# Attention's second product: weighed exponentials stationary, 17 columns of values and ones moving

## The reference, cut to what matters

```python
q, k, v = split_heads(h @ Wq.T), split_heads(h @ Wk.T), split_heads(h @ Wv.T)   # 8 heads of 16
scores = jnp.einsum('bhqd,bhkd->bhqk', q, k) / math.sqrt(HEAD_DIM)
scores = scores + jnp.log(adjacency + 1e-06)[:, None, :, :]
attn = jax.nn.softmax(scores, axis=-1)
out = jnp.einsum('bhqk,bhkd->bhqd', attn, v).transpose(0, 2, 1, 3).reshape(b, n, HIDDEN)
x = x + out @ Wo.T + bo            # h is the layer norm of x
```

## Time and profile before

| | |
|---|---|
| median of three runs | 2202.75 us (2199.62 to 2203.97) |
| the profiled execution | 2199.14 us, its span 2197.4 us |
| PE, DVE, ACT, POOL busy over the span | 77%, 56%, 38%, 35% |
| attention, steady part | 910 to 1270 us of the span, granted clock 1.00 |
| in 910 to 1270: PE, DVE, ACT busy | 273.12, 302.84, 163.89 us of 360 |

### The profile page before, as it was taken

The page is one execution under the profiler, slowest core; times in us unless marked ns, Lnnn a source line. Parts: engine busy times, 40 slices in busy tenths (PEclk is TensorE's granted clock), DMA queues, the critical chain, the costliest instruction groups (busy, mean ns, idle before and its releaser), DMA issues. The chain is left out here.

```text
span 2197.4 us, 44487 instructions
## 1 busy us (share of the span) xinstructions
PE 1691.7 (77%) x13042; PEld 1410.7 (64%) x13042; DVE 1234.2 (56%) x4542; ACT 824.8 (38%) x2531; POOL 764.8 (35%) x1118
## 2 busy tenths in 40 slices
PE   5567999987649966777777779935999957872996
PEld 4555777765639964566666657725999945661663
DVE  5673333349856756688888855512222248862543
ACT  2333444433336642344444434302655523330000
POOL 3430000013326745200000027773554424543565
PEclk8888999998879985799999989967999967665887
DMA  2100000001014420000000021114777752203331
GB/s 70 57 29 8 1 1 1 1 13 34 28 33 130 124 57 0 1 0 0 0 0 0 0 71 48 48 52 129 207 208 206 206 141 81 64 23 66 98 79 46
DMA packets 156776, 129.84 MB, mean 59 GB/s; under 512 B 27852, under 2 KB 131055, under 8 KB 156610
## 3 DMA queue, kind: packets, MB, share of 16 engines
q1 hardware_dynamic: 136130, 99.30, 16.6%
q0 software_dynamic: 13568, 25.90, 3.5%
q10 hardware_dynamic: 6912, 2.65, 0.6%
HBM read 96.51 MB, written 33.35 MB: 59 GB/s over the span
## 5 line engine op out<-in xcount | busy, mean ns | idle before, releaser
L1429 ACT ACTIVATE FEAT<-BANKS,EXP 128x128 f32<-128x128 f32 x544 | 155.0, 368 | 181.4 <-PE BANKS L1406 181.4
L1047 ACT ACTIVATE EXP<-BANKS,NEGMAX 128x128 f32<-128x128 f32 x512 | 139.0, 383 | 191.5 <-DVE NEGMAX L1059 191.5
L195 PE MATMUL BANKS<-ident,WA 128*128 128x128 f32 x256 | 62.8, 392 | 163.2 <-DVE WA L189 163.1
L1360 POOL DMA_INDIRECT scratch_made<-FEAT x136 | 130.2, 958 | 147.8 <-DVE FEAT L1489 144.8
L195 PEld LDWEIGHTS BANKS<-ident,WA 128*128 128x128 f32 x256 | 42.9, 199 | 174.2 <-DVE WA L189 136.8
L412 PE MATMUL BANKS<-FEAT,ident 128*128 128x256 f32 x588 | 150.0, 383 | 0.0
L1489 DVE TENSOR_TENSOR FEAT<-BANKS,B2BC 128x128 f32<-128x128 f32 x136 | 39.7, 292 | 194.5 <-PE BANKS L1415 194.5
L1406 PE MATMUL BANKS<-FEAT 128*128 128x128 f32 x1088 | 146.3, 278 | 2.4 <-DMA FEAT<-in_L_ffn_W1p 1.2
L1415 PE MATMUL BANKS<-AUX,FEAT 128*128 x1088 | 143.9, 275 | 0.4 <-ACT FEAT L1429 0.4
L1074 DVE RECIPROCAL WD<-BANKS 128x256 f32<-128x256 f32 x64 | 112.5, 1758 | 55.4 <-PE BANKS L1018 55.4
L1162 POOL DMA_INDIRECT scratch_sent<-FEAT,POS x128 | 123.7, 966 | 40.6 <-issue 37.8
(11 more groups left out here) (361 smaller groups left out, 4556.4 us busy)
## 6 DMA issues: line engine op xcount, KB each, us to landing
FEAT<-in_L_ffn_W1p SPq DMA_DIRECT2D x136, 256.0 KB
EXP<-in_L_ffn_W SPq DMA_DIRECT2D x128, 128.0 KB, 2.1
FEAT<-scratch_sent SPq DMA_DIRECT2D x136, 64.5 KB
STAGE<-in_adj SPq DMA_DIRECT2D x32, 256.0 KB, 3.0
EXP<-scratch_made SPq DMA_DIRECT2D x32, 256.0 KB
FEAT<-scratch_sent SPq DMA_DIRECT2D x96, 65.5 KB, 1.9
X<-in_x SPq DMA_DIRECT2D x16, 256.0 KB, 3.3
scratch_sent<-NONE SPq DMA_DIRECT2D x48, 65.5 KB, 3.9
```

What stands on the lines that cost most here:

```text
L195: last = pe.transpose(tile(ps, k), tile(src, k), ident[:])
L1047: last = act.activation(tile(EXS[:, par], 4 * k + n), tile(PS[j], c), ACT.Exp, bias=NEGMAX[:, par, 4 * k + n:4 * k + n + 1])
L1360: pool.indirect_dma_start(out=made2, out_offset=bass.IndirectOffsetOnAxis(ap=XI_I[:, t % R_IN, H:ROW2], axis=0), in_=YO[:, t % R_OUT, :], ...
L1429: last = act.activation(tile(HR[:, t % R_H], c), tile(PS[2 + t % 2], c), ACT.Gelu, bias=BT[:, c, t:t + 1])
```

## The change

`product` now holds a head's PTA tile (128x128) stationary and streams 17 columns past it: 16 of the values and one of ones, which VP now holds. The result is token-major, [128 tokens, 8 heads x 17] in ACC (136 columns of PS[7]). `divide` takes the reciprocal of 8 columns and multiplies with a broadcast. Since `output` needs features on the partitions, `flip` (PE) transposes the divided result into PS[6], `turned` (ACT) copies it to OTT, and `output` is one matmul with the plain Wo, into another part of PS[7]. Wo is loaded in one DMA and no longer in eight, and its zeroed buffer goes. The pipeline has a depth of five in place of three, and all steps are written out. The transposes no longer wait for `add`; `product` does. The rest of the diff adapts counts of waits.

```diff
-                for chunk in range(NC):
-                    for tile_at in range(HC):
-                        h = HC * (tile_at % 2) + 2 * chunk + tile_at // 2
-                        sp.dma_start(WoP[HP * tile_at:HP * tile_at + HD, chunk, :],
-                                     a["L2_gnn_Wo_T"][h * HD:(h + 1) * HD, :]).then_inc(s.w, 16)
+                sp.dma_start(WoT[:], a["L2_gnn_Wo_T"]).then_inc(s.w, 16)
...
+        HD1 = HD + 1
+        VP = EXP[:, 4 * SW:4 * SW + 2 * HEADS * HD1].rearrange("p (a h d) -> p a h d", a=2, h=HEADS)
+        OT = WC[:, :, 0:H]
+        OTT = WC[:, :, H:2 * H]
+        INV = WD[:, :, 0:HEADS]
+        ACC = PS[7][:, 0:HEADS * HD1].rearrange("p (h d) -> p h d", h=HEADS)
+        FLIP = PS[6][:, 0:T]
+        OUT = PS[7][:, 256:256 + H]
+        head_of = lambda slot: HC * (slot % 2) + slot // 2
...
                 def qk(i, par, half):
                     reused(pe, s.qk, i, 1)
+                    if i >= 4:
+                        pe.wait_ge(s.oc, i - 3)
...
                 def scores(i, par, half):
                     pe.wait_ge(s.qk, i + 1)
-                    reused(pe, s.ex, i, 1, 2)
                     for j in range(HC):
                         rows = slice(HP * j, HP * (j + 1))
+                        if i >= 1 and j % 2 == 0:
+                            pe.wait_ge(s.ex, 2 * (i - 1) + j // 2 + 1)
...
                 def transpose(i, par, half):
                     for k in range(2):
-                        if not isinstance(i, int) or i >= 1:
-                            pe.wait_ge(s.pTa, 2 * i)
-                            if not isinstance(i, int) or i >= 2:
-                                pe.wait_ge(s.x1, i - 1)
+                        if i >= 1:
+                            pe.wait_ge(s.pTa, 2 * (i - 1) + k + 1)
...
                 def product(i, par, half):
                     pe.wait_ge(s.vp, i + 1)
+                    pe.wait_ge(s.pTa, 2 * i + 2)
                     reused(pe, s.ot, i, 1)
-                    for k in range(NC):
-                        pe.wait_ge(s.pTa, 2 * i + k + 1)
-                        for what in range(2):
-                            for n in range(HC):
-                                h = HC * (n % 2) + 2 * k + n // 2
-                                lhsT = ones[:, 0:HP] if what else VP[:, par, h, :]
-                                at = (2 * what + k) * T
-                                last = pe.matmul(PS[7][HP * n:HP * (n + 1), at:at + T], lhsT,
-                                                 tile(PTA[:, par], 4 * k + n), start=True, stop=True)
+                    if i >= 2:
+                        pe.wait_ge(s.x1, i - 1)
+                    for slot in range(HEADS):
+                        h = head_of(slot)
+                        last = pe.matmul(ACC[:, h, :], tile(PTA[:, par], slot), VP[:, par, h, :], start=True, stop=True)
                     last.then_inc(s.pv, 1)
+                def flip(i, par, half):
+                    pe.wait_ge(s.ot, i + 1)
+                    pe.wait_ge(s.qk, min(i + 4, B))
+                    if i + 4 > B:
+                        pe.wait_ge(s.oc, i)
+                    pe.transpose(FLIP, OT[:, par], ident[:]).then_inc(s.oT, 1)
                 def output(i, par, half):
...
+                    pe.wait_ge(s.oc, i + 1)
+                    pe.wait_ge(s.ot, min(i + 2, B))
+                    reused(pe, s.x1, i, 1)
+                    pe.matmul(OUT, OTT[:, par], WoT[:], start=True, stop=True).then_inc(s.y, 1)
-                pipelined(pe, B, [(1, scores), (2, transpose), (0, qk), (2, product), (3, output)])
+                unrolled(B, [(1, scores), (4, flip), (5, output), (2, transpose), (3, product), (0, qk)])
...
-                pipelined(act, B, [(1, exps), (0, qk)])
+                def turned(i, par, half):
+                    act.wait_ge(s.oT, i + 1)
+                    reused(act, s.y, i, 2)
+                    act.copy(OTT[:, par], FLIP).then_inc(s.oc, 1)
+                unrolled(B, [(4, turned), (1, exps), (0, qk)])
...
-                    v.reciprocal(INV[:, par, 0:NC * T], PS[7][:, NC * T:2 * NC * T]).then_inc(s.inv, 1)
+                    v.reciprocal(INV[:, par], ACC[:, :, HD]).then_inc(s.inv, 1)
...
+                    v.tensor_tensor(OT[:, par].rearrange("p (h d) -> p h d", h=HEADS), ACC[:, :, 0:HD],
+                                    INV[:, par].unsqueeze(2).to_broadcast([P, HEADS, HD]), ALU.mult).then_inc(s.ot, 1)
...
-                pipelined(v, B, [(1, tops), (2, weigh), (2, divide), (3, add)])
+                unrolled(B, [(1, tops), (5, add), (2, weigh), (3, divide)])
```

More of the change, by code:

```diff
@@ L870, in program @@
         WvT = lb("WvT", [P, H])
-        WoP = lb("WoP", [P, NC, H])
+        WoT = lb("WoT", [P, H])
         bo_b = lb("bo_b", [P, H])
@@ L876, in _ @@
             def _(sp):
-                sp.wait_ge(s.zero, 3)
+                sp.wait_ge(s.zero, 2)
                 heads = lambda v: v.rearrange("i (h d) -> i h d", h=HEADS)
@@ L892, in _ @@
                 pool.memset(WkP[:], 0.0).then_inc(s.zero, 1)
-                pool.memset(WoP[:], 0.0).then_inc(s.zero, 1)
                 def dev(i, par, half):
@@ L904, in keep @@
                     pool.tensor_tensor(x, x, bo_b[:].unsqueeze(1).to_broadcast([P, G, H]), ALU.add).then_inc(s.x1, 1)
-                pool.wait_ge(s.w, 12 * 16)
+                pool.wait_ge(s.w, 5 * 16)
                 pipelined(pool, NG, [(0, dev), (2, keep)])
@@ L916, in norm @@
                     normalise(v, i, par, WA, MV, RS, 1, s.xn)
-                v.wait_ge(s.w, 12 * 16)
+                v.wait_ge(s.w, 5 * 16)
                 v.tensor_scalar(WqP[:], WqP[:], float(HD) ** -0.5, None, ALU.mult).then_inc(s.scaled, 1)
@@ L934, in values @@
                     last.then_inc(s.v_ps, 1)
-                pe.wait_ge(s.w, 12 * 16)
+                pe.wait_ge(s.w, 5 * 16)
                 pipelined(pe, NG, [(2, values), (1, xT)])
@@ L949, in _ @@
                 pipelined(act, NG, [(2, values), (1, xT)])
-        s = sems("att", "zero qk_ps qk score top ex pT pTa vp pv inv ot y x1")
+        s = sems("att", "zero qk_ps qk score top ex pT pTa vp pv inv ot oT oc y x1")
         SW = HEADS * T
+        HD1 = HD + 1
         EXS = EXP[:, 0:2 * SW].rearrange("p (a n) -> p a n", a=2)
         PTA = EXP[:, 2 * SW:4 * SW].rearrange("p (a n) -> p a n", a=2)
+        VP = EXP[:, 4 * SW:4 * SW + 2 * HEADS * HD1].rearrange("p (a h d) -> p a h d", a=2, h=HEADS)
         QKS = WA
-        OT, INV = WC, WD
-        VP = EXP[:, 4 * SW:4 * SW + 2 * HEADS * HP].rearrange("p (a h d) -> p a h d", a=2, h=HEADS)
+        OT = WC[:, :, 0:H]
[4 more added lines that the diff above has]
+        OUT = PS[7][:, 256:256 + H]
         NEGMAX = lb("NEGMAX", [P, 2, HEADS])
+        head_of = lambda slot: HC * (slot % 2) + slot // 2
         with nc.Block() as block:
@@ L963, in _ @@
             def _(pool):
-                pool.memset(VP, 0.0).then_inc(s.zero, 1)
+                pool.memset(VP, 1.0).then_inc(s.zero, 1)
                 pool.wait_ge(s.zero, 1)
@@ L971, in vp @@
                                      ).then_inc(s.vp, 1)
-                pipelined(pool, B, [(1, vp)])
+                unrolled(B, [(1, vp)])
             @block.tensor
@@ L1020, in product @@
-                    last.then_inc(s.pv, 1)
-                def output(i, par, half):
[L1023 to L1031, removed]
@@ L1073, in divide @@
                     v.wait_ge(s.pv, i + 1)
-                    v.reciprocal(INV[:, par, 0:NC * T], PS[7][:, NC * T:2 * NC * T]).then_inc(s.inv, 1)
+                    v.reciprocal(INV[:, par], ACC[:, :, HD]).then_inc(s.inv, 1)
                     v.wait_ge(s.inv, i + 1)
-                    reused(v, s.y, i, 2)
-                    v.tensor_tensor(OT[:, par, 0:NC * T], PS[7][:, 0:NC * T], INV[:, par, 0:NC * T], ALU.mult).then_inc(s.ot, 1)
+                    reused(v, s.oT, i, 2)
+                    v.tensor_tensor(OT[:, par].rearrange("p (h d) -> p h d", h=HEADS), ACC[:, :, 0:HD],
+                                    INV[:, par].unsqueeze(2).to_broadcast([P, HEADS, HD]), ALU.mult).then_inc(s.ot, 1)
                 def add(i, par, half):
                     v.wait_ge(s.y, i + 1)
-                    v.tensor_tensor(cols(X, i, H), cols(X, i, H), PS[4][:, 0:H], ALU.add).then_inc(s.x1, 1)
-                pipelined(v, B, [(1, tops), (2, weigh), (2, divide), (3, add)])
+                    v.tensor_tensor(cols(X, i, H), cols(X, i, H), OUT, ALU.add).then_inc(s.x1, 1)
+                unrolled(B, [(1, tops), (5, add), (2, weigh), (3, divide)])
         layer()
```

## The result

The changed kernel takes 2301.39 us (median of four runs, 2293.69 to 2313.37) against 2201.18 us (here the median of four runs of the kernel before): ratio 1.048, 95% interval 1.0443 to 1.0516. It is slower by 100 us, as forecast; 2280 was predicted, the range reached to 2330.

What follows compares the result with a forecast made beforehand. A cycle through DVE and PE was taken to bound the step; after the change, a chain through product's weight loads with clock partly lost. 2199.1 + 76.7 + 1 = 2277, on the median 2280; range 2222 to 2330.

Steps and rivals of the forecast that it cites:

- The old cycle runs through DVE and PE, 5.66: Attention step before: reciprocal, multiply, add, transposes, qk and product in one loop, 5.66 us; DVE alone about 4.9.
- Small terms: Attention step: new reciprocal 0.25 us and multiply 0.28 on DVE, ACT's added copy of 128 columns 0.35.
- Product 16 x 0.111 = 1.78: PE's product: 16 weight loads at 0.111 us each set its pace, 1.78 us at full clock, 0.72 more than before.
- Rival 2: Product's weight loads are hidden: product 0.44 us, step 4.74, time 2144, faster; chance 0.12.
- The cycle through the x1 wait and the copy, 6.08 and 9.56: New attention step: scores, maxima, add, product, qk, copy, scores in one chain, 6.08 us at full clock, 9.56 at half.
- The clock: Attention loses its granted clock of 1.00 in part: share 0.32 of the time at 1.2 GHz, range 0 to 0.6.
- the prediction's own formula: Mean attention step from time shares at both clocks: 1 / (0.68 / 6.08 + 0.32 / 9.56) = 6.88 us.
- the term of +76.7: Attention's 64 graphs at the mean step of 6.88 us: 440 us against 364.
- steps of 6.1 and of over 9 us: Sign that the forecast is right: attention steps of these lengths, with granted clock below 1.
- Rival 1: The attention's clock stays, all else as forecast: +26 us, 2230 on the median; chance 0.20.
- rival 3: Stuck at 1.2 GHz in most of the attention: step 8 to 9.56 us, time 2354 to 2452; chance 0.08.
- Around the loop: Outside the attention's steady steps: one Wo issue -3 us, deeper pipeline +4.0, loop control 0; together +1.

Runs made afterwards that it cites:

- short reciprocal: Kernel before with the reciprocal taken of 8 columns in place of 256 and one of them broadcast in the multiply: 2125.22 us, ratio 0.9675.
- add first: Changed kernel with DVE's order alone changed, add(j-5) ahead of tops(j-1), the maxima: 2250.88 us, ratio 1.0219 to the kernel before.
- qk first: Changed kernel with PE's order alone changed, qk(j) ahead of product(j-3): 2158.30 us, ratio 0.9737 to the kernel before.
- 136-column kernel: Changed kernel with each of product's eight matmuls streaming all 136 columns of VP in place of a head's 17: 2248.89 us, ratio 1.018 to the kernel before.

## Why the prediction was right, point by point

- *The old cycle runs through DVE and PE, 5.66.* Right: the short reciprocal gave 1.17 us a step and no more, because PE's own work (4.51, PE busy for 97%) is next.
- *Small terms.* On DVE the reciprocal 0.21 (0.25 taken) and the multiply 0.29 (0.28), on ACT turned 0.27 (0.35).
- *Product 16 x 0.111 = 1.78.* Right to the hundredth. Rival 2, hidden loads, is out: 8, 17 and 136 moving columns go at 0.111, 0.111 and 0.115 us a record at full clock. One sum in this part does not come out: 16 records at 1.06 / 32 = 0.033 are 0.53 and not 0.44, so rival 2 would have had a step of 4.83 and about 2150 us; nothing else hangs on it.
- *The cycle through the x1 wait and the copy, 6.08 and 9.56.* Measured 6.07 and 9.59. Both orders that cut it shorten the step (5.47 at full clock with add first, 4.68 with qk first).
- *The clock.* That the clock would be lost in part was right, and the runs show what loses it; how much was a guess by likeness. A share of 0.32 at 1.2 GHz was taken from the mildest of the layers of the earlier trace rows; it was 0.44. With 0.44 the prediction's own formula gives 1 / (0.56 / 6.08 + 0.44 / 9.56) = 7.24 us a step, about 99 us in all, and not the measured 6.90. The formula is wrong too: it takes it that 1.2 GHz slows all parts of a step alike. The step of 7.07 above has a clock of 0.76, 48% of its time at 1.2 GHz; the formula would make it 7.37. Low clock is cheap where PE would have waited in part anyway (from scores to product 2.45 us at full clock and 3.38 at half) and dear in product (1.78 and 3.42). So the term of +76.7, against 77.0 measured, came out by luck: two errors cancelled. The sign "steps of 6.1 and of over 9 us" was right for 17 of the 63; most steps span both levels. Rival 1 (clock stays) is what the 136-column kernel does, rival 3 never came.
- *Around the loop.* From SP's first issue to DVE's first work behind the weights it took 812.59 - 805.22 = 7.4 us before and 812.93 - 807.58 = 5.4 after: -2.0, not -3. The deeper pipeline cost 2.6 us up to the first reciprocal (DVE's first work to it 98.3 before, 100.9 after), and the attention's end is 0.8 shorter: +1.8, not +4.0. The two misses are of opposite sign; together -0.2 for the +1 taken.
- *What the sum lacked.* Layers whose code is unchanged: 24.7 of the 103.8 us behind the attention and 2.4 ahead of it (SP's first issue at 805.22 and 807.58; 1.8 of that is seen between two profiles of the kernel before, the second having it at 806.99). They were priced at nothing. For the profiled execution the sum gave 2277 and 2302.92 was measured: these layers are more than the 26 us between them. The range held them because it was wide, not because it had a term for them.

## What to carry to other kernels

Price a matmul by its weight loads as well as by its columns: with a 128x128 float32 stationary tile a record cost 0.111 us at full clock with 8 or 17 columns behind it, 0.115 with 136 and 0.163 with 192, so swapping the operands to make the moving side thin saved nothing and cost 0.72 us a step. When the work of one engine is shortened, follow the chain that closes the new step through all engines: here the last function of PE's list fed a copy for the first function of the next step, and moving that one entry was worth 143 us. Price the clock as well: the thin product kept it where PE ran without waits (qk first) and lost it where PE waited before and behind it, and a mean of step lengths over time shares is no safe way to say how much that costs.

## What the runs showed of the hardware

- More matmul work can be faster: 136 columns in place of 17 brought the granted clock from 0.78 to 1.00 and took 52 us off the program.
- The thin product alone doesn't lose the clock: with no waits beside it, it held 1.00 (PE busy 272.89 of 274 us).
- Lost clock costs by where it falls: a step with 48% of its time at 1.2 GHz took 7.07 us, where the mean of the rates of 6.07 and 9.59 gives 7.37.
- A matmul some 550 us behind the attention, with the same instructions around it, ran at 0.65 to 0.69 in four profiles of the old product and at 0.53 to 0.58 in ten of the new. Two kernels that differ in one layer differed by 19 us in another; why is open.
- The chip counts: the kernel before took 2199 to 2207 us (medians) on three chips and 2294.26 on a fourth.
